# The first mixture's numbering chain cut into four pieces between shared tiles, and its first routed tile transposed behind products

## The reference

```
logits = relu(xf @ Wr1 + br1) @ Wr2 + br2
gates = softmax(logits); tg, ti = top_k(gates, 2); tg = softmax(tg / 2)
out = silu(xf @ Ws1 + bs1) @ Ws2 + bs2                 # shared expert, all tokens
for e in range(8):                                      # eight experts, hidden size 1024
    h = silu(xf @ We1[e] + be1[e]) @ We2[e] + be2[e]
    out = out + sum(tg * (ti == e))[:, None] * h
x = x + out
```

## Time and profile before

| | us |
|---|---|
| median of 3 runs | 942.64 |
| lowest, highest | 940.12, 946.38 |
| the profiled execution, its own time | 940.64 |
| its span, first to last instruction | 938.7 |
| PE busy | 881.1 (94%) |
| DVE busy | 677.0 (72%) |
| ACT busy | 500.7 (53%) |
| mean granted TensorE clock | 0.967 |

### The profile page before, as it was taken

How to read it: one execution, slowest core, us unless ns; L and a number is a source line. 1 busy time by engine, 2 the same in 40 slices (tenths; PEclk the granted TensorE clock), 3 DMA queues, 4 the chain that set the end, 5 groups by cost and what they waited for, 6 DMA issues and landing times. The chain is left out here.

```text
span 938.7 us, 18032 instructions
## 1 busy us (share of the span) xinstructions
PE 881.1 (94%) x6325; PEld 810.1 (86%) x6325; DVE 677.0 (72%) x1301; ACT 500.7 (53%) x1014; POOL 199.9 (21%) x161
## 2 busy tenths in 40 slices
PE   8988999996979999999999999879997799999998
PEld 6877999995679999999999999659986578999997
DVE  4975999996674468888888889586776766655565
ACT  4642333332555576777777777534553544455543
POOL 8401322331015600323222432202221000000000
PEclk9989999998989999999999999798998899999999
DMA  8930000002222286676777786330000200100002
GB/s 303 297 101 1 1 1 1 1 1 70 76 68 97 103 286 225 224 224 224 224 224 218 219 264 203 80 117 1 1 1 1 90 24 3 40 27 22 0 1 90
DMA packets 47519, 97.45 MB, mean 104 GB/s; under 512 B 7298, under 2 KB 35172, under 8 KB 40932
## 3 DMA queue, kind: packets, MB, share of 16 engines
q1 hardware_dynamic: 38132, 85.23, 26.7%
q0 software_dynamic: 7152, 9.34, 5.0%
q10 hardware_dynamic: 2176, 2.10, 0.7%
HBM read 75.74 MB, written 20.91 MB: 103 GB/s over the span
## 5 line engine op out<-in xcount | busy, mean ns | idle before, releaser
L143 PE MATMUL e_ps_h<-e_xh,e_w1h 128*128 128x256 f32 (+1 forms) x496 | 142.7, 288 | 5.5 <-issue 5.5
L144 PE MATMUL e_ps_h<-e_xl,e_w1h 128*128 128x256 f32 (+1 forms) x496 | 140.0, 282 | 0.0
L145 PE MATMUL e_ps_h<-e_xh,e_w1l 128*128 128x256 f32 (+1 forms) x496 | 139.7, 282 | 0.0
L143 PE MATMUL e_ps_o<-e_w2h,e_hh 128*128 128x256 f32 x440 | 122.3, 278 | 0.0
L1758 ACT ACTIVATE e_hf<-e_ps_h,e_b1s 128x256 f32<-128x256 f32 (+1 forms) x248 | 97.9, 446 | 45.3 <-PE e_ps_h L145 43.9
L145 PE MATMUL e_ps_o<-e_w2h,e_hl 128*128 128x256 f32 x440 | 121.9, 277 | 0.0
L144 PE MATMUL e_ps_o<-e_w2l,e_hh 128*128 128x256 f32 x440 | 121.9, 277 | 0.0
L1638 POOL DMA_INDIRECT accumulated<-m_yo,m_token x39 | 74.5, 1909 | 199.4 <-ACT m_yo L1778 171.7
L850 POOL TENSOR_TENSOR at_pr<-at_pr,at_inv 128x1168 f32<-128x1168 f32 (+2 forms) x48 | 58.6, 1234 | 222.8 <-DVE at_inv L790 222.8
L143 PEld LDWEIGHTS e_ps_h<-e_xh,e_w1h 128*128 128x128 f32 x496 | 95.8, 193 | 5.7 <-issue 5.7
L144 PEld LDWEIGHTS e_ps_h<-e_xl,e_w1h 128*128 128x128 f32 x496 | 96.0, 194 | 0.0
(11 more groups left out here) (325 smaller groups left out, 2409.0 us busy)
## 6 DMA issues: line engine op xcount, KB each, us to landing
e_w1s<-in_m_w SPq DMA_DIRECT2D x24, 1024.0 KB
e_w2s<-in_m_w SPq DMA_DIRECT2D x24, 1024.0 KB, 7.3
slots_in<-zero SPq DMA_DIRECT2D x20, 258.0 KB, 8.8
e_xin<-slots_in SPq DMA_DIRECT2D x16, 258.0 KB, 4.9
as_wk<-in_a_wk SPq DMA_DIRECT2D x2, 1024.0 KB, 9.3
as_wv<-in_a_wv SPq DMA_DIRECT2D x2, 1024.0 KB, 11.7
X<-in_x SPq DMA_DIRECT2D x1, 2048.0 KB, 21.6
accumulated<-zero SPq DMA_DIRECT2D x8, 256.0 KB, 7.0
```

The costliest lines, as they stand in the source:

```text
L143: nc.tensor.matmul(out, lh, rh, start=start, stop=False)
L144: nc.tensor.matmul(out, lh, rl, start=False, stop=False)
L145: return nc.tensor.matmul(out, ll, rh, start=False, stop=stop)
```

## The change

`slots` is divided into three functions with the same operations: `tiles_of_experts`, `slots` and `experts_of_tiles`. `number` stays where it was, at the end of DVE's step 0; the other three are put between DVE's low halves of the hidden values of tiles 1 and 2. The transposes of tile 8 (the first routed one) move in PE's step 7 from ahead of the first product of tile 7 to behind it; ACT's and DVE's work on tile 8's tokens moves behind their work on tile 7's hidden values.

```diff
+    def tiles_of_experts(self, dve):
 ...
         dve.wait_ge(self.s_num, 1)
-        ends_p = c.prefix(dve, (pairs, self.pairs_a, self.pairs_b), E)
+        self.ends_p = c.prefix(dve, (pairs, self.pairs_a, self.pairs_b), E)
 ...
         link(dve, v.tensor_tensor(down[:], down[:], thr[:], ALU.add))
+    def slots(self, dve):
 ...
             v.tensor_copy(m.slots[:, i, :], self.mx[:, :, 0]).then_inc(self.s_k, 1)
+            dve.wait_ge(self.s_k, i + 1)
+
+    def experts_of_tiles(self, dve):
 ...
@@ tensor
-                if not static or j + 1 < J:
+                def transpose():
 ...
                     last.then_inc(s_tr, 1)
+
+                if not static or j + 1 < J and j != S - 1:
+                    transpose()
 ... (first product of tile j)
                         last.then_inc(s_m1, 1)
+                if static and j == S - 1:
+                    transpose()
 ... (second product of tile j - 1)
@@ scalar
-                    high_x(act, j + 1, 1 - q)
+                    if not static or j != S - 1:
+                        high_x(act, j + 1, 1 - q)
 ... (activations and high halves of tile j)
+                    if static and j == S - 1:
+                        high_x(act, S, 1 - q)
@@ vector
+                def routed_x(i, qi):
+                    wait(dve, s_xh, i + 1)
 ... (token numbers and gates of the tile)
+                    low_x(dve, i, qi)
 ...
                         low_w1(dve, unit(j + 1), q)
+                        if not static or j != S - 1:
+                            routed_x(j + 1, 1 - q)
 ... (in the loop over the four pieces, behind the low half of piece mp)
+                        if static and (j, mp) == (1, 0):
+                            router.tiles_of_experts(dve)
+                        if static and (j, mp) == (1, 1):
+                            router.slots(dve)
+                        if static and (j, mp) == (2, 0):
+                            router.experts_of_tiles(dve)
+                    if static and j == S - 1:
+                        routed_x(S, 1 - q)
 ...
                 if static and j == 0:
                     router.number(dve, ps_c)
-                    router.slots(dve)
```

More of the change, by code:

```diff
@@ L1453, in number @@
         v.tensor_reduce(self.units[:], self.over, AX.X, ALU.add).then_inc(self.s_num, 1)
[L1455 to L1459, removed]
+    def tiles_of_experts(self, dve):
+        v, c = self.nc.vector, self.chain
+        link = c.link
         pairs, units, room, thr, single, up, down = self.pairs, self.units, self.room, self.thr, self.single, self.up, self.down
         dve.wait_ge(self.s_num, 1)
-        ends_p = c.prefix(dve, (pairs, self.pairs_a, self.pairs_b), E)
-        link(dve, v.tensor_tensor(up[:], ends_p[:], pairs[:], ALU.subtract))
+        self.ends_p = c.prefix(dve, (pairs, self.pairs_a, self.pairs_b), E)
+        link(dve, v.tensor_tensor(up[:], self.ends_p[:], pairs[:], ALU.subtract))
         link(dve, v.tensor_scalar(room[:], up[:], -1.0, float(PAIRS), ALU.mult, ALU.add))
@@ L1469, in slots @@
         link(dve, v.tensor_scalar(up[:], up[:], float(ST), None, ALU.mult))
-        ends_s = c.prefix(dve, (single, self.single_a, self.single_b), E)
-        link(dve, v.tensor_tensor(down[:], ends_s[:], single[:], ALU.subtract))
+        self.ends_s = c.prefix(dve, (single, self.single_a, self.single_b), E)
+        link(dve, v.tensor_tensor(down[:], self.ends_s[:], single[:], ALU.subtract))
         link(dve, v.tensor_scalar(down[:], down[:], -float(P), float(PAIRS * ST + SINGLES * P - 1), ALU.mult, ALU.add))
         link(dve, v.tensor_tensor(down[:], down[:], thr[:], ALU.add))
+    def slots(self, dve):
+        v, m, link = self.nc.vector, self.m, self.chain.link
         row = lambda a: a[:].rearrange("p e a -> p a e").to_broadcast([P, NT, E])
-        link(dve, v.tensor_tensor(self.eq[:], self.slot[:], row(thr), ALU.is_lt))
-        link(dve, v.tensor_tensor(self.pro[:], self.slot[:], row(up), ALU.add))
-        link(dve, v.tensor_tensor(self.pro2[:], row(down), self.slot[:], ALU.subtract))
+        link(dve, v.tensor_tensor(self.eq[:], self.slot[:], row(self.thr), ALU.is_lt))
+        link(dve, v.tensor_tensor(self.pro[:], self.slot[:], row(self.up), ALU.add))
+        link(dve, v.tensor_tensor(self.pro2[:], row(self.down), self.slot[:], ALU.subtract))
         link(dve, v.tensor_tensor(self.pro[:], self.pro[:], self.pro2[:], ALU.subtract))
@@ L1486, in slots @@
             v.tensor_copy(m.slots[:, i, :], self.mx[:, :, 0]).then_inc(self.s_k, 1)
+            dve.wait_ge(self.s_k, i + 1)
+    def experts_of_tiles(self, dve):
+        v, g, m, L, link, tile_e = self.nc.vector, self.g, self.m, self.L, self.chain.link, self.tile_e
+        past_p, past_s = self.ex[0:1, 0:PAIRS], self.far[0:1, 0:SINGLES]
         tiles = lambda a, n: a[0:1].rearrange("p e a -> p a e").to_broadcast([1, n, E])
-        link(dve, v.tensor_tensor(past_p, tiles(ends_p, PAIRS), g.iota_tile[0:1, 0:PAIRS], ALU.is_le))
-        link(dve, v.tensor_tensor(past_s, tiles(ends_s, SINGLES), g.iota_tile[0:1, PAIRS:], ALU.add))
+        link(dve, v.tensor_tensor(past_p, tiles(self.ends_p, PAIRS), g.iota_tile[0:1, 0:PAIRS], ALU.is_le))
+        link(dve, v.tensor_tensor(past_s, tiles(self.ends_s, SINGLES), g.iota_tile[0:1, PAIRS:], ALU.add))
         link(dve, v.tensor_scalar(past_s, past_s, float(ROUTED - 1), None, ALU.is_le))
@@ L1804, in step @@
                 static = isinstance(j, int)
+                def routed_x(i, qi):
+                    wait(dve, s_xh, i + 1)
+                    n = i - S
+                    rows = slice(0, rows_of(i))
+                    for dst, col in ((token, TOKEN), (gate, GATE)):
+                        nc.vector.tensor_copy(dst[:, n, rows] if static else dst[:, bass.ds(n, 1), :].rearrange("p n a -> p (n a)"),
+                                              xin[:, qi, rows, col])
+                    low_x(dve, i, qi)
                 if not static or j + 1 < J:
@@ L1807, in step @@
                         low_w1(dve, unit(j + 1), q)
[L1808 to L1814, removed]
+                        if not static or j != S - 1:
+                            routed_x(j + 1, 1 - q)
+                    else:
+                        low_x(dve, j + 1, 1 - q)
                 if not static or 0 <= j < J:
```

## The result

The changed kernel takes 948.65 us (median of 22 runs, 941.88 to 956.63) where the kernel before, run beside it, takes 943.71 (22 runs, 938.61 to 949.64). The ratio is 1.0049, interval 1.0027 to 1.0070: slower by about 4.6 us. I had predicted 943.0, so +0.4 us, with a range up to 946.0. Of the 5.6 us between 943.0 and 948.65, 1.1 are the kernel before itself, which took 943.71 here and 942.64 in the runs that I started from. The profiled execution took 945.4 of its own (940.64 before), its span is 943.6.

A forecast was written before the change was run, and what follows sets the result against it. PE, busy 94% of the span, was taken as the bound. Of 7.7 us gained early, 2.4 stay after waits for loads; -2.4 + 2.8 for the clock gives +0.4, so 943.0 us, range 937.0 to 946.0.

The forecast's parts named there:

- The first cut: Slots in pieces on DVE: PE's stall at tile 2 falls from 5.5 us to 1.0, gaining 7.7 us.
- The scatter's start: POOL's first scatter starts 1.83 us later, at 274.3, because slots does.
- the moved transposes: Tile 8's transposes behind tile 7's first product in PE's step 7: cost nothing, wait for slots 1.4 us.
- The low clock behind tile 9: After PE's 3.9 us wait for tile 9's slots the clock falls, costing 2.8 us (bounds 0 and 2.8).
- stay within 1%: Whole kernel: time differs from before by no more than about 1% (9.4 us); chance 0.96.
- the landing of tile 9's slots: Tile 9's slots load takes 6.3 us (3.0 to 9.6) to land, at 344.3; PE waits 3.9 us.
- the chain: First scatter's start to SP's issue of tile 8's slots: stays 57.2 us, paced by POOL and DMA, not PE.
- rival 3: The scatter's chain grows, so step 8 starts later: 946.3 us at tile 9's upper landing bound; chance 0.15.
- the rival on the fast side: Loads of tiles 8 and 9 come in time and PE hardly waits: 936.9 or 936.3 us; chance 0.1.
- theory K: Later place of tile 8's W1 load lengthens the chain; issued sooner, chain 57 to 58 us, ratio 0.992 to 0.996.
- theory L: Chain longer from DMAs meeting PE, ACT, DVE at full pace, or chance: 60 to 63 us, ratio 0.994 to 0.998.

The follow-up runs named there:

- e1: Changed kernel with the numbering chain whole again in DVE's step 0, only tile 8's transposes moved: 941.88 us against 942.55, ratio 1.0017.
- e9: Changed kernel with 8 dummy matmuls on zeroes on PE ahead of each wait, for tile 8's and tile 9's slots: 947.29 us against 946.76, ratio 1.0031.
- e3: Changed kernel with SP's nine early loads issued behind W1 and slots of tile 9 and W2 of tile 8: ratio to before 1.0027.
- e4: Changed kernel with DVE's low half of tile 8's W1 moved behind the low halves of tile 7's hidden values: 946.07 us against 942.55, ratio 1.0049.
- e2: Changed kernel with tile 8's transposes ahead of tile 7's first product again, only the numbering pieces moved: 948.0 us against 942.55, ratio 1.0073.
- e15: Changed kernel measured once more without any edit: 946.28 us against 942.95, ratio 1.0037.
- e16: e14 with the expert numbers too right behind the slots, the whole chain behind tile 2's low-half tokens: 936.9 us against 945.73, ratio 0.9931.
- e5: Changed kernel with four scatters in flight in place of two: 954.66 us against 946.76, ratio 1.0107.
- e10: Changed kernel with e3, e4, tiles_of_experts and slots together behind tile 2's low-half tokens, four dummy matmuls at tile 8: 938.91 us against 942.95, ratio 0.9966.
- e14: e10 without the dummy matmuls: 937.29 us against 942.95, ratio 0.9948.
- e6: Kernel before the change with four scatters in flight in place of two, nothing else: ratio 1.0137.

## Why the prediction was wrong

**What held.** The first cut did what I said: step 2 fell by 7.75 us (I had 7.7), with 0.69 us of idle ahead of the second product of tile 1 (1.0) and a clock of 1.00. The scatter's start moved by 1.71 us behind tile 3 (1.83). No cost of the moved transposes shows (e1). The low clock behind tile 9 cost 2.7 us (2.8), and e9 shows that it was the clock and that the wait brought it down. The order of SP's queue was why tile 9's slots came late (e3). That the change would stay within 1% held too.

**What failed** are two terms. The larger: "From there the 32 scatters and their landing took 329.72 - 272.50 = 57.2 us, paced by POOL and by DMA and not by PE, so PE's gain doesn't shorten it". I took this length over as fixed. It was 60.5. The other is the landing of tile 9's slots, which I took as 6.3 us between bounds of 3.0 and 9.6: from the issue at 343.95 to PE at 351.73 it is 7.8. The 6.3 was no measurement. I called it the median with tile 9 between the others, but the profile has a landing for tiles 8 and 10 only, and 6.3 is the middle of their 3.0 and 9.6. By parts of the stretch:

| part of the stretch | before | predicted | measured |
|---|---|---|---|
| tile 3 to tile 4 | 20.26 | 12.6 | 12.51 |
| tile 4 to tile 9 | 57.84 | 63.2 | 67.73 |
| tile 9 to tile 10 | 11.55 | 14.3 | 14.21 |
| sum | 89.65 | 90.1 | 94.45 |

The miss of 4.4 us is the middle row's 4.5: 3.3 from the chain and 1.5 from the landing, less 0.1 each for the start of the scatter (5.67 in place of 5.76) and for SP's distance between the two loads (6.27 in place of 6.41). It is rival 3 of the prediction, "the scatter's chain grows", which I priced with 946.3, from the landing's upper bound alone and no growth of the chain at all. With what was measured, the sum is -2.4 + 3.3 + 1.5 - 0.2 for where step 8 begins and 2.7 for the clock, +4.9 us. The probability of 0.15 was too low for it: that 15 of 32 scatters waited on landings I counted for the rival on the fast side and not for this one. Nor did I ask what DVE would now do beside the last scatters, once its step 7 came earlier.

**Why the chain grew.** Shown: the last scatter took 2.96 us beside DVE's two-input operation of 2.28 and 0.97 when that one was moved away (e4). e2, e3 and e9 have it too (2.54, 2.35 and 2.50), and e15 a scatter of 2.81 us beside the same operation at another place of the chain. The Trainium skill (SBUF — State Buffer, SBUF: two separate sides) says that VectorE and GpSimd share a pair of ports which is held as an exclusive lock for a whole instruction, also by a VectorE operation with two SBUF inputs against a GpSimd one that reads SBUF. The trace fits it, with 0.97 against 2.96 us, if the issue of a scatter counts as such a read; no run here tests that. These 2.0 us are the largest piece of the 3.3, and e4 took them away without a gain, because the waits for landings were longer there. Not shown: why, with two in flight, POOL's waits for landings are 15.8 to 21.1 us in the kernels with the pieces moved and 15.1 and 15.6 in the two that leave them in step 0. The traces narrow it down a little. In each of these profiles the longest of those waits ends 4.0 to 7.8 us behind SP's issue of tile 8's W1, so the load of W1 holds the scatter up with and without the change. It is 2.77 us before:

```profile
281.24 0.97 POOL L1513 DMA_INDIRECT slots_in<-m_xn,m_slots  x1 [2.77 <-DMA slots_in<-m_xn,m_slots]
```

and in e16, which issues W1 as soon behind the first scatter as the kernel before (2.7 against 2.5 us), it is 4.26:

```profile
282.79 0.97 POOL L1520 DMA_INDIRECT slots_in<-m_xn,m_slots  x1 [4.26 <-DMA slots_in<-m_xn,m_slots]
```

So the place of W1's load (theory K) is not the whole reason. That its traffic now meets PE, ACT and DVE at full pace (theory L) no run tests by itself. The chain of e16, 59.4 us, lies between what the two expect.

**Why four in flight failed.** I had argued that what shortens the chain is won by PE. It is not so where four scatters in flight slow PE: the chain gave 12 us (e5) and PE lost more. Only the two quantities together say what a faster scatter is worth.

**What the loss was, then.** PE gained 7.75 us early. The chain is the real bound of the mixture's beginning: its start moved back by 1.7 us, it grew by 3.3, and PE comes to its end ahead of time and pays for the wait with its clock. Cures that start the chain sooner and let tile 9's load follow at once (e10, e14, e16) turned +4.6 us into a gain of 3.2 to 6.5; four in flight, which attacks its pace, did not. All three also move the low half of W1 (e4), and the sooner start was never run by itself, so its own share is not shown.

## What to carry to other kernels

A stall that is removed ahead of a longer chain is worth only what that chain leaves: find the transfer that the next steps wait for, and put first on the engine what starts it, then what fills PE. Keep the operations between the chain's start and its first DMA together, and behind only that one operation for which PE would wait, as in e10, e14 and e16. And count a TensorE wait amid dense matmuls at its length plus what the clock takes, unless another wait follows that absorbs it: behind waits of 2.95 us (e4), 3.27 (e14), 3.54 (changed) and 5.52 (before) the low clock took about another 1.6, 2.7, 2.7 and 2.8 us.

## What I had not expected of the hardware

- With four indirect scatters of 128 rows in flight instead of two, PE sat idle between ordinary matmuls by 0.2 to 1.7 us at a time, and the kernel before became 1.4% slower (e6), though from its first to its last start the scatter was 9.9 us faster (44.8 in place of 54.7).
- A VectorE operation of 2.28 us with two inputs took an indirect DMA's issue on POOL from 0.97 to 2.96 us. The issues that stand beside 128x512 ones took 0.97 to 1.64.
- The other way round, a tiny VectorE operation beside a memset of 3.73 us on POOL took 4.45 us in place of 0.61, in three of the 14 profiled executions and not in the others, where the memset stood beside it too.
- How long a wait must be for the clock to fall is no fixed number. Behind waits of 2.32 us (e16) and 2.19 us (e9, behind the dummies) it stayed at 1.00, behind 2.01 us at tile 9 in e15, 8.6 us after a wait of 9.51, it was 0.67, and that step took 13.33 us in place of 11.55 (stretch behind it, columns as above):

```profile
353.80:358.00 4.20, 4.20 (x26) 4.20 (x27) 1.74 (x2) 3.13 (x5) 0.00 (x0) 0.67 1.03 426
```

- Dummy products for 3.6 us in a wait of 5.8 us kept the clock at 1.00 behind it (e9).
